# A graph layer on one core: experts on tiles of the rows routed to them, in place of all eight experts on every tile

## The reference, cut to what matters

```python
xn = _layernorm(x)
x = x + _L0_gnn_ref(xn, ...) + _L0_mix_ref(xn[None], ...)[0]
x = x + _L0_ffn_ref(_layernorm(x)[None], ...)[0]
...
# in _L0_ffn_ref, tokens is the normalised x
logits = tokens @ router_w.T                       # 8 experts
probs = softmax(logits)
rw, re = top_k(probs, 2)
rw = rw / rw.sum(-1)
combine = zeros((N, 8)).at[arange(N)[:, None], re].set(rw)
out = tokens
for e in range(8):
    h = gelu(tokens @ w1[e] + b1[e])               # 256 x 256, exact gelu
    y = h @ w2[e] + b2[e]
    out = out + combine[:, e:e + 1] * y
```

## Time and profile before

| | us |
|---|---|
| Median of 3 runs | 1601.41 |
| Lowest, highest | 1600.71, 1602.5 |
| Span of the profiled execution | 1685.8 |
| PE busy in it | 1601.8 |
| DVE busy | 1340.2 |
| ACT busy | 961.4 |
| POOL busy | 999.6 |

### The profile page before, as it was taken

The page is one execution under the profiler, slowest core; times in us unless marked ns, Lnnn a source line. Parts: engine busy times, 40 slices in busy tenths (PEclk is TensorE's granted clock), DMA queues, the critical chain, the costliest instruction groups (busy, mean ns, idle before and its releaser), DMA issues.

```text
span 1685.8 us, 31748 instructions
## 1 busy us (share of the span) xinstructions
PE 1601.8 (95%) x10509; PEld 1451.7 (86%) x10509; DVE 1340.2 (79%) x3389; ACT 961.4 (57%) x2156; POOL 999.6 (59%) x1111
## 2 busy tenths in 40 slices
PE   7999999999999989998789999999999999999998
PEld 6888888777877878786689999999999999999998
DVE  7888565577777777775569999889999999999985
ACT  4444322345555555554566767667766777666764
POOL 4533322766676666673766767666766666666630
PEclk9999999999999999998999999999999999999999
DMA  9776656677877877787633333333333333333320
GB/s 295 267 258 246 235 226 238 222 242 242 259 249 242 257 228 252 238 265 271 203 98 100 108 104 112 100 102 101 117 101 106 101 116 100 99 109 110 104 62 10
DMA packets 127076, 290.50 MB, mean 172 GB/s; under 512 B 21271, under 2 KB 49724, under 8 KB 126914
## 3 DMA queue, kind: packets, MB, share of 16 engines
q1 hardware_dynamic: 86068, 177.19, 28.9%
q0 software_dynamic: 39952, 110.13, 24.1%
q10 hardware_dynamic: 894, 1.16, 0.2%
HBM read 149.49 MB, written 138.90 MB: 171 GB/s over the span
## 4 chain that ended last, share of the span: by engine, by line
PE 67%; DVE 12%; issue 8%; ACT 6%; another core or an unknown queue 3%; POOL 2%; DMA 1%; SPq 0%; DVEq 0%; ACTq 0%; POOLq 0%
PE bank L1821 52%; PE bank L2025 3%; PE bank L2026 2%; PE bank L1865 2%; PE bank L1866 2%; ACT mh L1030 2%; DVE ml L1606 2%; DVE ml_a L1357 1%; POOL stg L814 1%; PE bank L1977 1%; DVE ht L1722 1%; DVE xres L1736 1%; ACT raw L1086 1%; DVE stg L1224 1%
## 5 line engine op out<-in xcount | busy, mean ns | idle before, releaser
L814 POOL DMA_INDIRECT stg<-table,idxcur x495 | 530.6, 1072 | 263.9 <-issue 172.9
L1821 PE MATMUL bank<-wreg,xt 128*128 128x512 f32 x2352 | 589.9, 401 | 7.3 <-issue 6.5
L1821 PEld LDWEIGHTS bank<-wreg,xt 128*128 128x128 f32 x2352 | 438.6, 191 | 100.5 <-issue 11.4
L696 POOL DMA_INDIRECT raw<-table,idxa x297 | 302.5, 1018 | 147.3 <-issue 85.4
L1821 PE MATMUL bank<-tt,wreg 128*128 128x256 f32 (+1 forms) x2400 | 319.5, 282 | 0.0
L1821 PE MATMUL bank<-wreg,ht 128*128 128x256 f32 x2352 | 314.7, 283 | 0.4 <-DVE ht L1722 0.2
L1821 PEld LDWEIGHTS bank<-tt,wreg 128*128 128x128 f32 x2400 | 296.4, 189 | 2.9
L1821 PEld LDWEIGHTS bank<-wreg,ht 128*128 128x128 f32 x2352 | 293.2, 189 | 0.9 <-DVE ht L1722 0.4
L1086 ACT ACTIVATE raw<-bank,cols 128x256 f32<-128x256 f32 (+1 forms) x400 | 164.4, 462 | 132.7 <-remote 72.6
L1224 DVE COPY stg<-bank 128x512 f32<-128x512 f32 x196 | 134.2, 686 | 110.4 <-PE bank L1821 76.1
L1606 DVE SCALAR_TENSOR_TENSOR ml<-stg,nrm,mh 128x256 fp32r<-128x256 f32 x455 | 195.5, 478 | 13.4 <-ACT mh L1030 12.8
(11 more groups left out here) (244 smaller groups left out, 2086.9 us busy)
## 6 DMA issues: line engine op xcount, KB each, us to landing
table<-stg SPq DMA_DIRECT2D x196, 512.0 KB
kv_d<-kvs SPq DMA_DIRECT2D x49, 256.5 KB
xt_d<-xt SPq DMA_DIRECT2D x49, 256.0 KB
xtp<-xt_d SPq DMA_DIRECT2D x24, 512.0 KB
stg<-table,idxcur POOLq DMA_INDIRECT x495
sk<-kv_d SPq DMA_DIRECT2D x24, 256.5 KB
out_x<-xres SPq DMA_DIRECT2D x24, 256.0 KB
xres<-in_x POOLq DMA_DIRECT2D x23, 256.0 KB, 4.0
```

The source lines that it names most:

```text
L696: pool.indirect_dma_start(ring_a[:, r * EARLY + j, :], None, table[0:LIMIT, :], bass.IndirectOffsetOnAxis(ap=idxa[:, at:at + 1], axis=0)). ...
L814: pool.indirect_dma_start(stg[:, (s % 4) * SUP + j, :], None, table, bass.IndirectOffsetOnAxis(ap=idxcur[:, at:at + 1], axis=0)).then_inc( ...
L1821: mm = pe.matmul(dst, stat(a, c), mov(b, c), start=(n == 0), stop=(n == 3 * chunks - 1))
```

## The change: what it does

The expert steps of a pair go. In their place each row is sent to a region in HBM (`routed_d`) for each of its two experts, and the experts run on whole tiles of 128 such rows, 105 in all, which is the number that suffices for any routing. The steps with `~` in the slots belong to tile `f = 4i - 19 + s // 2`, less one for `~... 1`: four tiles a round, the first in round 4.

- `CHOOSE`, `RANK` and `PLACE` count on DVE and PE, for pair `i-2`, how many rows each expert has so far, and so find the place of each row in its expert's region. `send` on POOL writes the rows there by indirect DMA: two tiles by two experts, four a pair, 1044 bytes a row (the row, the two weights, the two experts, its own number). `send_seeds` adds eight once, at pair 0, so that no row of a region is unset.
- `PICK` chooses on DVE the expert with most rows waiting, for four tiles a pair and for the last 16 at the end. SP (`load_tiles`) and PE (`experts`) read the choice into registers, SP loads the tile and its expert's two biases.
- `TX`, `X_HI`, `X_LO` (transpose and split), `L1` (first product, with its bias as a seventh matmul), `GELU`, `TH`, `H_HI`, `H_LO`, `L2`, `Y` (scale by the weight): the experts on one tile. The rows are the stationary side in both products, the weights are addressed by the register.
- `add_out` on POOL adds the 128 results into the output by indirect DMA with an addition. Each waits until the one before has landed (`y_st`), since a row can be in both.
- `store_pair` stores x plus its normalised form before the experts' part is there, right after `NORM`.
- The loop runs five more rounds for the tiles that are left after the last pair. Constants for the routing are made on POOL at tile 6 of the first phase, and a triangular matrix at round 1.

```diff
-    AHEAD = 2 * X
-    BEGUN = 1
+    TOPK = 2
+    TILES = (TOPK * N + X * (P - 1)) // P
+    PER_PAIR = 4
+    FULL = PER_PAIR * (NP - 2) + 1
+    XC = C + 5
+    W_AT, E_AT, ID_AT = C, C + 2, C + 4
+    REGION = NT * P + P
+    DUMP = X * REGION
+    RING_X, RING_Y = 6, 4
+    LEAD, LAG = 19, 7
...
+        def picks_of(q):
+            return range(FULL, TILES) if q == NP else range(max(0, PER_PAIR * (q - 2) + 1), PER_PAIR * (q - 1) + 1)
+        def sent_by(p):
+            return 16 * (X + 2 * TOPK * (p + 1) - (TOPK if p == NP else 0))
...
             def store_pair(p, nt):
-                sp.wait_ge(y_add, 2 * X * p + X * nt + AHEAD)
+                sp.wait_ge(acc_act, 2 * p + nt)
+                if p:
+                    sp.wait_ge(out_st, 16 * p)
...
+            def load_tiles(q):
+                if not picks_of(q):
+                    return
+                sp.wait_ge(pick_dve, q)
+                sp.wait_ge(sent, sent_by(q))
+                if q == 1:
+                    sp.wait_ge(w_lo, 8)
+                for f in picks_of(q):
+                    row = sp.value_load(rowi[0:1, f:f + 1], min_val=0, max_val=DUMP - P)
+                    e = sp.value_load(expi[0:1, f:f + 1], min_val=0, max_val=X - 1)
+                    if f >= RING_X:
+                        sp.wait_ge(y_st, 16 * (f - RING_X + 1))
+                    if f >= 3:
+                        sp.wait_ge(tile_in[f % 3], 32 * (f // 3))
+                    sp.dma_start(xin[:, f % RING_X, :], routed_d[bass.ds(row, P), :]).then_inc(tile_in[f % 3], 16)
+                    if f >= 4:
+                        sp.wait_ge(ffn_mm, count_of(f - 4, SECOND))
+                    sp.dma_start(halves(brow[32 * (f % 4):32 * (f % 4) + 2, :]), bias_d[bass.ds(e, 1)].rearrange("a h c -> (a h) c")
+                                 ).then_inc(tile_in[f % 3], 16)
...
-            for p in range(2, NP):
-                load_pair(p, 2)
-                store_pair(p - 2, 2)
-            load_pair(NP, 1)
-            store_pair(NP - 2, 2)
-            store_pair(NP - 1, 2)
-            store_pair(NP, 1)
+            for i in range(1, NP + 3):
+                if 2 <= i <= NP:
+                    load_pair(i, 2 if i < NP else 1)
+                if i - 1 <= NP:
+                    store_pair(i - 1, 2 if i - 1 < NP else 1)
+                load_tiles(i - 2)
...
+            def send(p, nt, k):
+                if k == 0:
+                    pool.wait_ge(pos_dve, p + 1)
+                    if p:
+                        pool.wait_ge(sent, sent_by(p - 1))
+                for a in range(nt):
+                    pool.indirect_dma_start(routed_d, bass.IndirectOffsetOnAxis(ap=posi[:, p % 2, 2 * k + a:2 * k + a + 1],
+                                                                                axis=0),
+                                            tn2[p % 2][:, a, :], None).then_inc(sent, 16)
+            def send_seeds():
+                for e in range(X):
+                    pool.indirect_dma_start(routed_d, bass.IndirectOffsetOnAxis(ap=seedi[:, e:e + 1], axis=0),
+                                            tn2[0][:, 0, :], None).then_inc(sent, 16)
+            def add_out(f):
+                for q in range(1, NP + 1):
+                    if f == picks_of(q)[0]:
+                        pool.wait_ge(out_st, 16 * (q + 1))
+                pool.wait_ge(ffn_act, count_of(f, SECOND))
+                if f:
+                    pool.wait_ge(y_st, 16 * f)
+                pool.indirect_dma_start(out, bass.IndirectOffsetOnAxis(
+                    ap=xin[:, f % RING_X, ID_AT:ID_AT + 1].bitcast(I32), axis=0),
+                    yout[:, f % RING_Y, :], None, compute_op=ALU.add).then_inc(y_st, 16)
...
-            gathers(0, 8)
-            gathers(1, 8)
-            for i in range(2, NP):
-                gathers(i, 8)
-            gathers(NP, TAIL_GROUPS)
-            roots2(NP - 1, 2)
-            roots2(NP, 1)
+            added = 0
+            for i in range(NP + 8):
+                groups = 8 if i < NP else TAIL_GROUPS if i == NP else 0
+                if i == 1:
+                    triangle()
+                for s in range(8):
+                    ready = (8 * i + s - 2 * LEAD - (LAG if i <= NP else 4)) // 2
+                    while added < min(ready + 1, TILES):
+                        add_out(added)
+                        added += 1
+                    if 2 <= i <= NP + 2 and s in (5, 6):
+                        send(i - 2, 2 if i - 2 < NP else 1, s - 5)
+                        if i == 2 and s == 6:
+                            send_seeds()
+                    if s < groups:
+                        gather(i, s, groups)
+                    if (i, s) in ((NP, 7), (NP + 1, 4)):
+                        roots2(i - 1, 2 if i == NP else 1)
...
+            def X_HI(f):
+                act.wait_ge(ffn_turn, count_of(f, FIRST))
+                if f >= 2:
+                    act.wait_ge(ffn_mm, count_of(f - 2, FIRST))
+                act.copy(xf[f % 2][:, HI].rearrange("p c n -> p (c n)"), bank[2][:, 0:C]).then_inc(ffn_hi, 1)
+            def GELU(f):
+                act.wait_ge(ffn_mm, count_of(f, FIRST))
+                if f >= 2:
+                    act.wait_ge(ffn_turn, count_of(f - 2, SECOND))
+                act.activation(hid[:, f % 2, :], bank[6][:, 0:C], ACT.Gelu).then_inc(ffn_act, 1)
...
+            def Y(f):
+                act.wait_ge(ffn_mm, count_of(f, SECOND))
+                act.wait_ge(w_ready, f + 1)
+                if f >= RING_Y:
+                    act.wait_ge(y_st, 16 * (f - RING_Y + 1))
+                act.activation(yout[:, f % RING_Y, :], bank[7][:, 0:C], ACT.Copy,
+                               scale=wcol[:, f % RING_X:f % RING_X + 1]).then_inc(ffn_act, 1)
...
+            def CHOOSE(p, nt):
...
+                ch.link(dve, dve.tensor_tensor(
+                    chosen[:, :, 0:nt], iota8[:].unsqueeze(1).unsqueeze(1).to_broadcast([P, TOPK, nt, X]),
+                    tn2[b][:, 0:nt, E_AT:E_AT + 2].rearrange("p a k -> p k a").unsqueeze(3).to_broadcast([P, TOPK, nt, X]),
+                    ALU.is_equal))
...
+                dve.tensor_tensor(acnt[:, 0:nt], chosen[:, 0, 0:nt], chosen[:, 1, 0:nt], ALU.add).then_inc(chosen_dve, 1)
...
+            def PLACE(p, nt):
+                b = p % 2
+                dve.wait_ge(rank_mm, p + 1)
+                ch.inc(dve.tensor_tensor(places[:, 0:nt], bank[5][:, 0:nt * X].rearrange("p (a e) -> p a e", e=X),
+                                         a_base.unsqueeze(1).to_broadcast([P, nt, X]), ALU.add))
...
+                ch.link(dve, dve.tensor_tensor(picked[:, :, 0:nt], chosen[:, :, 0:nt],
+                                               places[:, 0:nt].unsqueeze(1).to_broadcast([P, TOPK, nt, X]), ALU.mult))
+                spots = posf.rearrange("p (k a) -> p k a", k=TOPK)[:, :, 0:nt]
+                ch.link(dve, dve.tensor_reduce(spots, picked[:, :, 0:nt], AX.X, ALU.add))
...
+                dve.tensor_tensor(a_base, bank[5][:, 2 * X:3 * X], a_base, ALU.add).then_inc(pos_dve, 1)
...
+            def PICK(p, nt):
+                dve.wait_ge(pos_dve, p + 1)
+                todo = list(picks_of(p))
+                while todo:
+                    fs, todo = todo[:X], todo[X:]
+                    n, a, z = len(fs), fs[0], fs[-1] + 1
+                    ch.link(dve, dve.tensor_tensor(backlog, a_base, a_done, ALU.subtract))
+                    ch.link(dve, dve.scalar_tensor_tensor(
+                        out=cand, in0=backlog.unsqueeze(2).to_broadcast([P, X, X]), scalar=float(X * X),
+                        in1=a_cand.rearrange("p (e j) -> p e j", e=X), op0=ALU.mult, op1=ALU.add))
+                    ch.link(dve, dve.max(best, cand.rearrange("p e j -> p (e j)")))
+                    ch.link(dve, dve.tensor_copy(besti[:, 0:n], best[:, 0:n]))
...
+                    ch.link(dve, dve.tensor_tensor(which[:, 0:n], iota8[:].unsqueeze(1).to_broadcast([P, n, X]),
+                                                   expf[:, a:z].unsqueeze(2).to_broadcast([P, n, X]), ALU.is_equal))
...
+                    if p < NP:
+                        ins = dve.scalar_tensor_tensor(out=rowi[:, a:z], in0=ahead_of[:, 0:n], scalar=float(P),
+                                                       in1=first[:, 0:n], op0=ALU.mult, op1=ALU.add)
...
+            def X_LO(f):
+                r = f % RING_X
+                dve.wait_ge(tile_in[f % 3], 32 * (f // 3 + 1))
+                if f >= RING_X:
+                    dve.wait_ge(ffn_act, count_of(f - RING_X, SECOND))
+                ch.link(dve, dve.scalar_tensor_tensor(out=weighed[:, r], in0=xin[:, r, E_AT:E_AT + 2],
+                                                      scalar=expf[:, f:f + 1], in1=xin[:, r, W_AT:W_AT + 2],
+                                                      op0=ALU.is_equal, op1=ALU.mult))
+                if f < FULL:
```

(68 more changed lines are left out.)

460 lines of the change are left out of this document (244 added, 216 removed).

## The result

The changed kernel takes 2074.93 us (median of four runs, 2074.01 to 2076.43), the kernel before 1601.2 beside it: ratio 1.2948, 95% interval 1.2929 to 1.2967. The forecast was 1820, 1700 to 1930. The direction was right, the size was not: the profiled span is 2073.6 where the sum said 1918.

What follows compares the result with a forecast made beforehand. PE bounded the kernel before; POOL, at 41.3 us a pair against 34.0, would bound the changed one. Gathers ending at 1779 us plus a 139 us drain gave a 1918 span, times 0.950 about 1820; range 1700 to 1930.

Steps and rivals of the forecast that it cites:

- POOL's price: On POOL, each gather, send and add was priced at 1.37 us, so a full pair needs 41.3 us.
- I charge no stall: On POOL, the waits of sends and adds were taken as already met, so no time was added.
- No other engine comes near: In a full pair, POOL's 41.3 us was taken as the period, with every other engine well below it.
- Even twice 20.5 stays under 41.3: In the pairs, PE's 20.5 us of work, even doubled, would stay below POOL's 41.3 us.
- the sign of being right: In the pairs, PE would be busy near half of the 41 us from one index copy to the next.
- The drain: After the last gather, 24 tiles at 5.0 us each, plus PICK, first load and last add: 139 us.
- what costs nothing: Work taken as hidden, including 16 register loads ahead of the last tiles, at most 9 us, partly under the tiles' loads.
- Times 0.950: The 1918 us span was scaled by 0.950 from profile to runs, giving 1822, stated as 1820.
- dear scatters: Rival on POOL: scatters cost up to 2.7 us each, giving 2158 or 2050; chance of dearer than 1.37: 0.13.
- the 0.30 pause: Rival: the pause after POOL's indirect DMAs is the trace's own, giving 1615 to 1650 us; chance 0.10.
- a free scatter: Rival: a scatter costs POOL nearly nothing, pairs go to 28 us on DVE, time 1546 at zero price; faster 0.05.
- The two rules: Skill rules: DVE blocking POOL, unused, would give 37.9 us a pair; a 3.7 us add would make the drain 19 us less.

Runs made afterwards that it cites:

- the run at 1866: Changed kernel with messages first, PLACE early, roots ahead of slot 6's third gather, expert numbers read one at a time, idle matmuls in the drain only: 1865.86 us.

## Why the prediction was wrong, step by step

- **POOL's price** came out right as a total, in part by luck: 28 x 1.37 + 2.9 = 41.3 was forecast, and where POOL stands nowhere a pair takes 40.4 to 40.8. But in the run at 1866 a gather or send takes 1.30 and an add 1.98 (inside the bounds of 0.77 and 2.7), and everything else 1.5 a pair, not 2.9: the adds were 2.4 us a pair too cheap in the forecast, the rest 3.1 too dear.
- **"I charge no stall"** is the step that failed, and the largest term: POOL waits 10.2 us a pair, and the 18 pairs take 147 us more than 41.3 each. I checked what the sends wait for, but neither that PLACE was behind at POOL's pace, nor which of POOL's other instructions now stood behind the sends and who waited for those. With the roots earlier 139 us go.
- **"No other engine comes near"** failed more quietly: by busy time it holds (PE 34.7 us a pair, DVE 26.3), but the chain of handoffs through PE, ACT and DVE takes 42.3 us, just above POOL's need. It hid there until the ring was open.
- **"Even twice 20.5 stays under 41.3"** holds as throughput (PE is 70% busy at a clock of 0.62, and not near half of the time, as the sign of being right had it). The low clock lengthens that chain too: six matmuls take up to 1.58 us in it. What this costs a pair was not measured apart; idle matmuls won back 0.94 us.
- **The drain** at 5.0 a tile is mis-sized: 6.41 at 1.2 GHz, as the paragraph on the clock allowed (4.2 and 2.3 more, 36 us in all), which I left out of the sum. At the high clock most adds start 4.5 to 4.9 apart, inside 4.0 to 5.4. PE starts 26 first products after the last gather, not 24; the 16 reads, which I had put under what costs nothing, cost 7.7. The drain took 201 us, not 139. Of the 62, 26 tiles at 6.41 for 24 at 5.0 make 47, by estimate, and the reads 7.7; the other 7 or so were not taken apart.
- **"Times 0.950"** was wrong: the sum started from a hampered execution's first phase (its pairs were longer too, 34.2 for 33.0), and the factor then cut POOL's part as well, which was never long. It took 96 us off, where the first phase was 58 too long. With pair 1 ending at 787.5 the sum gives 1860. Messages first, with the drain's clock up, has a span of 1862, and so near only by luck: its pairs 2 to 23 take 20 us less than the sum has for them, and what follows pair 23 takes 23 more.
- **The rivals**: dear scatters (2158 or 2050) would have come near the time by a cause that isn't there, since sends and adds took 1.28 and 1.96; the 0.30 pause is real, since the profiled span has it and agrees with the runs (2073.6 and 2074.93); a free scatter is out.
- **The two rules**: a gather's mean falls from 1.074 to 0.979 us as LOW goes. That agrees in direction with the Trainium skill (SBUF — State Buffer, "Who interferes with whom"), where a DVE instruction with two SBUF inputs contends with a GpSimd one that reads SBUF. It shows no more: DVE was also less busy (54% for 90%), no run separates the two, and with messages first and DVE 65% busy the mean is 1.020. The add lands 3.9 us after the start of its issue in the median (3.7 to 5.1 in the drain at the high clock). My estimate of 3.7 from the Trainium skill (DMA: Bandwidth & Descriptors, "Anatomy of one DMA — SWDGE (gpsimd) path") was close to that. But the next add starts another 0.75 us later at the earliest, so start to start the adds need 4.5, and they and not the 4.2 chain would set a tile. "No transfer here shows so short a landing" was a misreading: in the trace of before the one load of 106 KB from POOL landed after 3.3 us.

## What to carry to other kernels

When instructions are put into an engine's queue, list not only what they wait for but every later instruction of that queue that another engine waits for, and look in the trace how much slack it had: here 0.12 us. Two engines that wait for each other once a round make a ring, whose length is the sum of both arcs, and neither engine looks full. Behind the chain that is opened the next one may stand close: here 49.5 us a pair by the ring, 42.3 by the handoffs, 40.4 to 40.8 by POOL's own work. Take a second profile before scaling by the difference between a profile and the runs.
